# Router logits of x from host-turned rows: four batches at once in four column groups and one transpose, in place of four 14-column products a batch

## The reference, cut to what matters

```python
x = x + tanh(g_xattn) * attention(layernorm(x), ctx, ctx)      # 16 heads, causal mask
h = layernorm(x)
logits = h @ router_w                                          # 4096 rows x 14
assignments = argmax(logits, axis=-1)
weights = softmax(logits)[assignments]
hid = gelu(h @ w1[assignments] + b1[assignments])
x = x + tanh(g_ffn) * weights * (hid @ w2[assignments] + b2[assignments])
```

## Time and profile before

| | |
|---|---|
| median of 3 runs | 473.49 us (473.02 to 473.74) |
| span of the profiled execution | 479.0 us |
| steps 0 to 34 | from the start to about 290 us |
| PE, DVE, ACT busy in 120 to 160 us | 40.00, 37.38, 36.40 of 40 us |

### The profile page before, as it was taken

The page is one execution under the profiler, slowest core; times in us unless marked ns, Lnnn a source line. Parts: engine busy times, 40 slices in busy tenths (PEclk is TensorE's granted clock), DMA queues, the critical chain, the costliest instruction groups (busy, mean ns, idle before and its releaser), DMA issues.

```text
span 479.0 us, 16593 instructions
## 1 busy us (share of the span) xinstructions
PE 453.8 (95%) x4775; PEld 371.5 (78%) x4775; DVE 350.8 (73%) x1128; ACT 314.3 (66%) x1481; POOL 303.2 (63%) x668
## 2 busy tenths in 40 slices
PE   8999999999999999999999998959799999999991
PEld 4888888888888888888888887849699997545550
DVE  3668999899999999999999987645336443645640
ACT  2689999899899899898998997231222222344440
POOL 5476587687876877877868676566445555445321
PEclk9899999999999999999999999988989999999997
DMA  6274556211112112111120079795778887798500
GB/s 222 66 240 139 160 164 176 53 42 47 56 33 59 40 33 66 33 44 55 34 68 15 14 203 246 235 210 161 254 249 281 280 249 235 240 344 251 167 10 6
DMA packets 38765, 65.68 MB, mean 137 GB/s; under 512 B 12457, under 2 KB 27055, under 8 KB 38704
## 3 DMA queue, kind: packets, MB, share of 16 engines
q1 hardware_dynamic: 26272, 35.33, 25.3%
q10 hardware_dynamic: 7424, 19.60, 12.9%
q0 software_dynamic: 5008, 10.01, 7.6%
HBM read 55.84 MB, written 9.99 MB: 137 GB/s over the span
## 4 chain that ended last, share of the span: by engine, by line
PE 86%; DVE 4%; another core or an unknown queue 2%; issue 2%; DMA 2%; ACT 1%; SPq 1%; POOL 0%; POOLq 0%; DVEq 0%
PE bank L1566 11%; PE bank L1635 11%; PE bank L1474 9%; PE bank L1482 7%; PE bank L1625 7%; PE bank L1574 6%; PE bank L1558 6%; PE bank L1702 6%; PE bank L1517 5%; PE bank L1496 5%; PE bank L1615 2%; PE bank L1621 2%; PE bank L1553 2%; PE bank L1461 2%
## 5 line engine op out<-in xcount | busy, mean ns | idle before, releaser
L857 ACT ACTIVATE arena<-bank,negmax 128x128 f32<-128x128 f32 x512 | 179.6, 402 | 13.7 <-DVE negmax L1136 13.6
L857 ACT ACTIVATION_READ_ACCUMULATOR arena<-bank,negmax 128x1 f32 x512 | 123.6, 241 | 0.0
L1136 DVE TENSOR_REDUCE negmax<-bank 128x4 f32<-128x512 f32 x128 | 84.4, 681 | 12.5 <-PE bank L1558 12.2
L610 POOL DMA_INDIRECT out<-g_out,g_name x39 | 39.0, 1000 | 66.5 <-DVE g_name L1091 51.3
L1566 PE MATMUL bank<-C,arena 128*128 128x128 f32 x512 | 78.9, 276 | 0.1
L815 ACT ACTIVATE hid_t<-bank,w_ring 128x128 f32<-128x128 f32 x100 | 28.5, 370 | 70.3 <-PE bank L1474 44.5
L1566 PEld LDWEIGHTS bank<-C,arena 128*128 128x128 f32 x512 | 63.2, 142 | 9.1 <-ACT arena L857 0.8
L1635 PE MATMUL bank<-arena 128*128 128x128 f32 x512 | 68.1, 276 | 1.3 <-DMA arena<-ctxt 1.0
L1635 PEld LDWEIGHTS bank<-arena 128*128 128x128 f32 x512 | 62.2, 192 | 3.1 <-issue 2.4
L1474 PE MATMUL bank<-g_xt,w_ring 128*128 128x128 f32 x400 | 52.3, 287 | 8.1 <-DVE g_xt L1079 8.1
L1474 PEld LDWEIGHTS bank<-g_xt,w_ring 128*128 128x128 f32 x400 | 50.2, 202 | 9.7 <-issue 9.4
(11 more groups left out here) (179 smaller groups left out, 1000.7 us busy)
## 6 DMA issues: line engine op xcount, KB each, us to landing
w_ring<-w1b ACTq DMA_DIRECT2D x15, 642.0 KB
w_ring<-w1b ACTq DMA_DIRECT2D x14, 514.0 KB
W<-w SPq DMA_DIRECT2D x14, 512.0 KB
arena<-w1b SPq DMA_DIRECT2D x14, 512.0 KB, 5.1
w_ring<-w1b SPq DMA_DIRECT2D x10, 642.0 KB
token_rows<-rows SPq DMA_DIRECT2D x32, 129.0 KB, 3.9
arena<-x SPq DMA_DIRECT2D x32, 128.0 KB
arena<-ctxt SPq DMA_DIRECT2D x31, 128.0 KB, 2.3
```

What stands on the lines that cost most here:

```text
L610: pool.indirect_dma_start(out=out_rows, out_offset=bass.IndirectOffsetOnAxis(ap=g_name[:, r, 0:1], axis=0), in_=g_out[:, r, :], in_offset= ...
L857: ins = act.activation(probs[:, q, v, :], bank[q][:, v * P:(v + 1) * P], ACT.Exp, bias=negmax[:, b.par, h:h + 1], accum_out=rsum[:, b.par, ...
L1136: dve.tensor_reduce(negmax[:, b.par, q * HQ:(q + 1) * HQ], bank[q][:, :].rearrange("p (v k) -> p v k", v=HQ), axis=AX_X, op=ALU.max, negat ...
```

## The change

What L1621 computed for one batch in every step is computed for four batches in one of four steps, from x itself.

- The host hands over x a second time, turned (`xt`, columns of x on partitions, 512 KB for four batches). SP loads it into the last slot of `w_ring`, for the first group before the steps, later at k = 1.
- At k = 2 PE's `multiply_x_logits` has the router as stationary operand, padded from 14 to 32 columns (`rw_wide`), and the four batches as moving ones: eight products, in four column groups of PSUM partitions. DVE's `keep_x_logits` copies the 128x128 result to SBUF after `residual` of the same step.
- At k = 3 PE turns it back in one transpose, and DVE's `biased_x_logits` adds the router's bias for four batches at once.
- `dense` loses L1621, `residual` loses L1168, POOL loses `given_logits`.
- The scores at k = 3 wait for the copy as well, those at k = 0 for the biased logits, since bank 0 holds both.

```diff
-        rw_sb = part(DC * E).rearrange("p (c n) -> p c n", c=DC)
+        rw_wide = part(DC * SPAN).rearrange("p (c n) -> p c n", c=DC)
+        rw_sb = rw_wide[:, :, 0:E]
+        x_t = w_ring[:, R - 1, 0:GROUP * D].rearrange("p (k c s) -> p k c s", k=GROUP, c=DC)
...
+            def load_xt(t):
+                hold(x_logits_done, t.round)
+                sp.dma_start(x_t.rearrange("p k c s -> p (k c s)"),
+                             xt[:, bass.ds(t.round * GROUP, GROUP), :].rearrange("p b n -> p (b n)")
+                             ).then_inc(xt_loaded, 16)
...
             sp.dma_start(wd_turned_sb, wd_turned).then_inc(router_loaded, 16)
+            load_xt(Batch(0, 0))
             run_steps(sp, step)
...
-            def given_logits(c):
...
             def residual(c, at=bank[0]):
                 dve.wait_ge(dense_done, c.n + 1)
-                dve.wait_ge(given_ready, c.n + 1)
-                dve.scalar_tensor_tensor(scaled[:, :], at[:, XLOGIT:XLOGIT + E], rstd[:, c.slot, 2:3],
-                                         given[:, c.slot, :], ALU.mult, ALU.add).then_inc(logits_scaled, 1)
...
+            def keep_x_logits(t):
+                dve.wait_ge(x_logits_done, t.round + 1)
+                dve.tensor_copy(x_logits_t[:, :], bank[0][:, XLOGIT:XLOGIT + P]).then_inc(x_logits_kept, 1)
...
             def dense(c, at=bank[0]):
-                for ch in range(DC):
-                    pe.matmul(at[:, XLOGIT:XLOGIT + E], xh_t[:, c.back(2).slot, ch, :], rw_sb[:, ch, :],
-                              start=(ch == 0), stop=(ch == DC - 1))
                 pe.wait_ge(attn_ready, c.n + 1)
...
+            def multiply_x_logits(t):
+                pe.wait_ge(xt_loaded, (t.round + 1) * 16)
+                for ch in range(DC):
+                    for k in range(GROUP):
+                        ins = pe.matmul(bank[0][SPAN * k:SPAN * (k + 1), XLOGIT:XLOGIT + P], rw_wide[:, ch, :],
+                                        x_t[:, k, ch, :], start=(ch == 0), stop=(ch == DC - 1))
+                ins.then_inc(x_logits_done, 1)
...
                     wait(pe, logits_summed, b.n - 1)
+                    if t.k % GROUP == 3:
+                        pe.wait_ge(x_logits_kept, t.round + 1)
+                    if t.k % GROUP == 0:
+                        wait(pe, x_logits_ready, t.round)
                     scores(b)
```

More of the change, by code:

```diff
@@ L44 @@
 WIDE = D + E
-XLOGIT = D + 16
+XLOGIT = D + 32
+GROUP = 4
+SPAN = P // GROUP
 ROUND = 1.5 * 2.0 ** 23
@@ L132, in batch, with flamingo_kernel @@
     return Batch(0, n)
-def flamingo_kernel(nc, x, ctxt, gates, wq, wk, wv, wd, wd_turned, bqk, bv, bd, bd_column, rw, w1b, b1, w2, consts, out):
+def flamingo_kernel(nc, x, xt, ctxt, gates, wq, wk, wv, wd, wd_turned, bqk, bv, bd, bd_column, rw, w1b, b1, w2, consts, out):
     token_rows = nc.dram_tensor("token_rows", [TOK + P, ROW], F32, kind="Internal").ap()
@@ L306, in flamingo_kernel @@
         router_ready = sem("router_ready")
-        logits_scaled = sem("logits_scaled")
-        given_step = sem("given_step")
-        given_ready = sem("given_ready")
+        xt_loaded = sem("xt_loaded")
+        x_logits_done = sem("x_logits_done")
+        x_logits_kept = sem("x_logits_kept")
+        x_logits_turned = sem("x_logits_turned")
+        x_logits_ready = sem("x_logits_ready")
         centre_ready = sem("centre_ready")
@@ L635, in row_scale @@
                 inverse_rows(h)
-            def given_logits(c):
[L639 to L645, removed]
             def centre(h):
-                pool.tensor_scalar(from_mean[:, 1, :], rw_sum[:, :], rows[:, h.slot, MEAN:RSTD], None,
+                pool.tensor_scalar(from_mean[:, :], rw_sum[:, :], rows[:, h.slot, MEAN:RSTD], None,
                                    ALU.mult).then_inc(centre_ready, 1)
@@ L679, in step @@
                     replicate(c)
-                    if c.static and c.n == 0:
-                        pool.wait_ge(router_ready, 1)
-                    given_logits(c)
                 if h.ok():
@@ L746, in _ @@
             row_scale(batch(29))
-            given_logits(batch(30))
             fetch(2, 2, early_rows)
@@ L753, in _ @@
             row_scale(batch(30))
-            given_logits(batch(31))
             fetch(4, 4, early_rows)
@@ L1321, in step @@
                     residual(c)
+                if t.ok() and t.k % GROUP == 2:
+                    keep_x_logits(t)
+                if t.ok() and t.k % GROUP == 3:
+                    biased_x_logits(t)
                 if b.ok():
@@ L1347, in step @@
                     dve.wait_ge(stats_done, a.n + 1)
-                    wait(dve, given_ready, a.n - 3)
+                    wait(dve, rstd_ready, a.n - 3)
                     dve.sem_inc(vector_waits, 1)
@@ L1627, in dense, with turn_x_logits @@
                 ins.then_inc(dense_done, 1)
+            def multiply_x_logits(t):
[5 more added lines that the diff above has]
+                ins.then_inc(x_logits_done, 1)
+            def turn_x_logits():
+                pe.transpose(bank[0][:, XLOGIT:XLOGIT + P], x_logits_t[:, :], ident).then_inc(x_logits_turned, 1)
             def step(t):
@@ L1684, in step @@
                     router_bias()
+                if t.ok() and t.k % GROUP == 2:
+                    if t.static and t.n == 2:
+                        pe.wait_ge(out_w_loaded, 16 * 2)
+                    multiply_x_logits(t)
+                if t.ok() and t.k % GROUP == 3:
+                    turn_x_logits()
                 if c.ok():
@@ L1835 @@
         "x": x,
+        "xt": np.asarray(x).reshape(B, P, DC, P).transpose(3, 0, 2, 1).reshape(P, B, DC * P),
         "ctxt": np.asarray(ctx_1024).reshape(B, P, DC, P).transpose(3, 0, 2, 1).reshape(P, B, DC * P),
```

30 lines of the change are left out of this document (21 added, 9 removed).

## The result

The changed kernel takes 483.25 us, median of 4 runs (482.36 to 485.98); the kernel before took 473.62 (473.02 to 473.93) beside it. The ratio is 1.0205, interval [1.0169, 1.0242]: about 2% slower, 9.6 us. The forecast was 480.1, range 476 to 484, chance of slower 0.88.

The account below looks back on a forecast made before the run. DVE's chain to the normalised attention, not a full PE, was taken to set the step. Terms 4.4 + 1.1 + 2.0 - 0.2 - 0.7 = +6.6 took the span from 479.0 to 485.6; 5.5 lower gave 480.1, range 476.0 to 484.0.

Parts of the forecast that it names:

- the dear product: Rival, loop: product takes 1.02 us in each of seven steps, L1621's removal gains nothing; +4.6, 484.9 us; chance 0.06.
- Wait for xt, +4.4: Start-up: PE waits for xt until 14.65, so the keys start at 16.25 and not 11.83; +4.4 us.
- PE's clock, +2.0: Start-up: after standing still 5.0 us, PE works some 4 us at half speed; +2.0 us.
- Copy behind the gate folding, +1.1: Start-up: scores of batch 0 wait for DVE's copy behind `fold_gate`; first maximum at 16.95, not 15.87; +1.1 us.
- The loop, -0.2: Batch loop: -1.8 us from L1621 gone, +1.7 from the product in seven steps, taken as -0.2 after rounding.
- the forecast 0.08 a step: Loop: removing L1621 gains 0.08 us in each of 23 steps without the product, -1.8 us.
- The forecast's 0.6: Loop, k = 2: the product takes 0.6 us in place of L1621's 0.36, +0.24 in each of seven steps.
- The tail, -0.7: Tail: two more L1621 go from `dense` of the last batches, 0.35 us each; -0.7 us.
- PE's rows count in full: Rival, loop: PE, not DVE's chain, sets the step; loop gives -6.5 us, total 473.8; chance 0.11.
- The cheap start-up: Rival, start-up: clock stays at 1.00 and the copy hides, only the xt wait is left; 477.0 us; chance 0.13.

Follow-up runs that it names:

- second profile of before: The kernel before, unchanged, run once more to profile another execution: 474.6 us, with a span of 472.8.

## Why the prediction was right, and where its sizes were off

Between the profiles of after and of before that lie near their medians, 483.8 and 474.6 us, the 9.2 us divide so: to the scores of batch 1, 31.36 - 22.25 = +9.1; from there to the last scores, 264.26 - 261.31 = +2.95; behind them 186.04 - 189.22 = -3.2; outside the span 2.1 - 1.8 = +0.3. The sign of the forecast and its mechanism in the start-up hold; the loop it had wrong. That 483.25 lies inside the range, 0.75 from its end, is in part luck. Against the forecast the start-up cost 1.6 more (9.1 for 7.5), the loop 3.1 more, and the 0.3 outside the span were not foreseen; the tail gave back 2.5 more than its 0.7, for no reason that the forecast had. By this account the time would have been near 485.7 without these 2.5. And the range reached up to 484 only because it was drawn half-way to the dear product, a rival that did not come.

The prediction also took its span from a long execution: 485.6 was due for the span and 481.7 came, and the 5.5 between span and median that it carried over belonged to that one execution. The terms:

**Wait for xt, +4.4: right.** The product starts at 14.50 (forecast 14.65), and with 1.6 us for product and values at full speed the keys would have stood at 16.1, +4.3. The runs with the product behind the keys and in step 3 take this away.

**PE's clock, +2.0: right in kind, too small ahead of the scores.** From 14.50 to the keys 2.88 us passed and not 1.6, and from the keys to the end of L1674 3.74 (17.38 to 21.12) where before had 2.14 up to the scores (11.83 to 13.97): 2.9 us. But the profile of before had a fall of its own in step 3, which the forecast did not set against it: 10.53, where the second profile without it has 8.98, 1.55 us.

**Copy behind the gate folding, +1.1: right for the first maximum.** The scores are 1.59 late. But the first maximum, which stood 1.90 behind them in the earlier trace rows (13.97 to 15.87), now follows 1.38 behind (22.71 to 24.09), so that 1.07 reaches it. Step 3 is shorter by 0.33 for a clock that stays up in both (8.65 for 8.98).

Together with 4.3 and 2.9 the 1.59 makes the 8.74 from 13.97 to 22.71; less the 1.88 by which step 3 is shorter (10.53 to 8.65) it is 6.9 against the profile that the prediction read, where it had 7.5.

**The loop, -0.2: the term that failed, +2.6 against the first profile of before and +2.9 against the second.** By steps, against the second: fifteen of the steps without the product (t = 4 to 28, but for t = 11, 15, 19 and 23) give 1.0 back, 0.6 at k = 0, 0.3 at k = 1 and 0.1 at k = 3, which is near the forecast 0.08 a step. The seven with the product cost 2.3 and not 1.7: 0.32 in each of six and not 0.24, and 0.40 at t = 30. The forecast's 0.6 was to hold the way into the column groups and out of them as well. The product itself takes 0.57, but with the 0.09 that the transposes ahead of it lose, and the 0.02 behind, it is 0.68. That this lies on the path was right: L1621 had cost about 0.1 of its 0.36 there (8.67 against 8.55 at k = 0), the product costs 0.44 (8.99 against 8.55).

Not foreseen at all is the rest, where the forecast expected 0.6 back. The four steps t = 11, 15, 19 and 23, each just ahead of an iteration of the loop, cost 0.7 (9.07 to 9.22 against 8.79 to 9.34, and up to 9.98 in other executions). Steps t = 29 and 31 to 33 cost 1.0. Of that, 0.65 (t = 29) show in two of the eight profiles that have the changed loop without an edit; 0.4 to 0.5 at t = 32 show in all eight. In t = 32 stands neither the product nor the copy nor the addition; DVE's first maximum starts there 2.49 us behind the scores (278.03 to 280.52), and 1.81 in the second profile of before (266.46 to 268.27). What makes it late, and what lengthens the four steps, stays open.

**The tail, -0.7: right for the two products, and 3.2 in all.** From the last scores of the loop at 283.57 to the dense product of batch 31 and the expert row behind it, in the second profile of before:

```profile
299.61 0.51 PE L1621 MATMUL bank<-arena 128*128 128x14 f32 x4
299.97 1.16 PE L1625 MATMUL bank<-arena 128*128 128x270 f32 x4
300.97 1.72 PE L1474 MATMUL bank<-g_xt,w_ring 128*128 128x128 f32 x14
```

And in the changed kernel, with the last scores at 295.62:

```profile
311.44 1.07 PE L1642 MATMUL bank<-arena 128*128 128x270 f32 x4
312.35 1.83 PE L1494 MATMUL bank<-g_xt,w_ring 128*128 128x128 f32 x15
```

17.40 against 16.73: 0.67. The whole way from the last scores to the end took 185.3 to 188.4 us in the runs with the changed loop, and 189.2 and 192.85 in the two profiles of before. The 2.5 beyond the 0.67 stay open. A part may lie in the clock: behind the last scores the 400 rows of the first expert layer (L1474, now L1494) were busy 51.3 us in the second profile of before and 48.9 in the changed kernel. Nor did the forecast have the 0.3 outside the span, in every run with xt as an input (2.1 to 2.8 against 1.8). Where they come from wasn't tried.

**The rivals.** That PE's rows count in full falls by the run with L1621 put back (2.65 us where 8.3 were due). The cheap start-up falls by the rows at half speed. The dear product falls by its 0.58 where 1.02 was assumed.

## What to carry to other kernels

Ask of each product on a full engine what it waits beside: work ahead of a wait that binds is nearly free (L1621's 0.36 us were worth 0.07 to 0.12), and work that replaces it is charged for all that outlasts the wait (0.44 for the product). Fewer, larger products of the same work can so cost more than many small ones that lie in waits. Work that needs a new transfer should not stand in the start-up ahead of work that could already run; the same product in the next step, behind the scores, cost 7.65 us less.

## What the runs showed of the hardware that was not expected

One kernel can have its TensorE clock fall in the start-up in one execution and not in the next: before fell to 0.50 from 19.1 to 22.5 us in one profile, with PE counted as busy all the time, and stayed at 1.00 there in the other, where step 3 took 1.55 us less. Five of the runs with a changed start-up or without L1621 show it in the same step 3, which then takes 10.2 to 10.8 instead of 8.65 us. The other six of the changed kernel and its variants don't; in four of these the clock had been low just before, behind the wait for xt. The Trainium skill, on the page "TensorE: Matmul & The Clock Gate", section What's actually happening, says that the number of slow matmuls at a kernel's start varies between runs of one kernel. The traces agree that it varies, though the falls in step 3 come 19 us and more behind the start of the span. A saving of 1 to 2 us in a start-up can be taken back by it, as it was for the copy in the two profiled executions. In the 35 runs of before that stand beside the experiments, the 18 with a mean granted clock of 0.989 or more took 470.7 to 474.3 us, the 7 with 0.985 or less 473.6 to 477.0.

PE's changes between forms of a product have a price that rows show. In step t = 18 of the changed kernel a row starts 0.16 to 0.17 us ahead of the modelled end of the row before it where both have the same form, and 0.07 to 0.08 where the form changes (128x128, 128x32 or 32x128). A change costs some 0.09 us by that; the product brings two of them into a step, and L1621 brought none.
